# The Mamba layer's u times B on TensorE for three of sixteen states, with the h*C sum two slots behind the scan

## The reference

```python
def _selective_scan(x, dt, Bm, Cm, A, D):
    dA = jnp.exp(dt[..., None] * A)
    dBx = (dt * x)[..., None] * Bm[:, :, None, :]
    def step(h, inputs):
        dA_t, dBx_t, C_t = inputs
        h = dA_t * h + dBx_t
        y = jnp.einsum('bdn,bn->bd', h, C_t)
        return (h, y)
    ...
    return jnp.swapaxes(ys, 0, 1) + x * D[None, None, :]
```

## Time and profile before

| | before |
|---|---|
| time, median of 3 runs | 2807.88 us (2804.88 to 2809.41) |
| the profiled execution's own time | 2813.86 us |
| its span, first to last instruction | 2811.9 us |
| granted TensorE clock, mean of the span | 0.947 |
| the scans' stretch, about 334 to 1297 us of the span | some 963 us |

### The profile page before, as it was taken

How to read it: one execution, slowest core, us unless ns; L and a number is a source line. 1 busy time by engine, 2 the same in 40 slices (tenths; PEclk the granted TensorE clock), 3 DMA queues, 4 the chain that set the end, 5 groups by cost and what they waited for, 6 DMA issues and landing times. The chain is left out here.

```text
span 2811.9 us, 35676 instructions
## 1 busy us (share of the span) xinstructions
PE 2458.8 (87%) x10516; PEld 1557.5 (55%) x10516; DVE 2198.9 (78%) x4237; ACT 1732.2 (62%) x3055; POOL 1438.5 (51%) x1514
## 2 busy tenths in 40 slices
PE   7997587878888888877899599979999999997999
PEld 5876243333334334324677388855555555546887
DVE  7997589989999999997899555458877778755444
ACT  5876565557556666644777355536676767665555
POOL 2474698888888988885277450033232323310000
PEclk8999698999999999999999699989999999998999
DMA  2356222222222222222157310000000000001000
GB/s 83 79 158 122 69 76 70 72 69 74 68 73 76 75 74 74 75 76 66 35 149 137 95 34 1 1 15 1 1 1 1 1 1 1 1 1 42 8 8 15
DMA packets 99497, 146.06 MB, mean 52 GB/s; under 512 B 13036, under 2 KB 50540, under 8 KB 99124
## 3 DMA queue, kind: packets, MB, share of 16 engines
q1 hardware_dynamic: 82196, 98.60, 12.3%
q0 software_dynamic: 16608, 44.78, 7.5%
q10 hardware_dynamic: 512, 0.53, 0.1%
HBM read 124.98 MB, written 18.87 MB: 51 GB/s over the span
## 5 line engine op out<-in xcount | busy, mean ns | idle before, releaser
L1809 POOL TENSOR_TENSOR a_hc<-a_H,a_cb 128x512 f32<-128x512 f32 x512 | 619.6, 1231 | 136.6 <-DVE a_H L1672 129.2
L1464 PE MATMUL a_Y<-a_hc,ident 128*128 128x512 f32 x1024 | 541.7, 640 | 58.4 <-POOL a_hc L1809 49.8
L2165 ACT ACTIVATE a_pt<-a_W 128x512 f32<-128x512 f32 (+3 forms) x768 | 346.2, 496 | 202.8 <-PE a_W L2065 199.0
L1590 ACT ACTIVATE a_dA<-a_dt,a_aneg 128x512 f32<-128x512 f32 x512 | 342.8, 714 | 191.8 <-POOL a_dt L1828 100.6
L1464 PEld LDWEIGHTS a_Y<-a_hc,ident 128*128 128x128 f32 x1024 | 183.8, 197 | 313.2 <-POOL a_hc L1809 218.8
L1696 DVE TENSOR_TENSOR a_BX<-a_u,a_BX 128x1024 f32<-128x1024 f32 x256 | 308.2, 1209 | 38.3 <-PE a_BX L1398 27.3
L1672 DVE TENSOR_TENSOR_SCAN a_H<-a_dA,a_H,a_BX 128x512 f32<-128x512 f32 x256 | 312.1, 1261 | 2.5 <-ACT a_dA L1590 2.5
L2388 POOL TENSOR_SCALAR_AFFINE_SELECT a_pt<-a_pt 128x512 f32<-128x512 f32 x128 | 90.9, 710 | 423.1 <-ACT a_pt L2165 423.1
L1672 DVE TENSOR_TENSOR_SCAN a_H<-a_dA,a_BX 128x512 f32<-128x512 f32 x256 | 296.4, 1200 | 0.5 <-POOL a_hc L1809 0.5
L2251 DVE CUSTOM_DVE_ANT_0 a_masked<-a_W,a_mask 128x384 f32<-128x384 f32 (+3 forms) x512 | 231.7, 486 | 80.0 <-PE a_W L2052 77.8
L2065 PE MATMUL a_W<-a_Q,a_K 128*128 128x512 f32 (+3 forms) x768 | 283.6, 385 | 1.7 <-ACT a_pt L2165 1.6
(11 more groups left out here) (328 smaller groups left out, 5471.6 us busy)
## 6 DMA issues: line engine op xcount, KB each, us to landing
a_cb<-a_crow SPq DMA_DIRECT2D x256, 256.0 KB, 3.3
m_orows<-m_yt SPq DMA_DIRECT2D x46, 256.0 KB, 2.5
t_wst<-ternary_w SPq DMA_DIRECT2D x22, 256.0 KB, 2.9
m_xrows<-m_xn SPq DMA_DIRECT2D x16, 256.0 KB, 2.3
m_xg<-m_xrows,m_gidx POOLq DMA_INDIRECT x184, 3.3
out<-x SPq DMA_DIRECT2D x8, 256.0 KB, 2.3
m_wg<-moe_ws SPq DMA_DIRECT2D x2, 516.0 KB, 4.5
a_hc<-mamba_conv_rows SPq DMA_DIRECT2D x1, 1024.0 KB, 5.2
```

The source lines that it names most:

```text
L1464: pe.matmul(Y[:, h, :], ident[:], hc[:, g % HCRING, :], start=False, stop=v == NS - 1).then_inc(s_y, 1)
L1590: act.activation(dA[:, G % ARING, :], dt[:, b % 2, h, :], ACT.Exp, scale=aneg[:, d, h, v:v + 1]).then_inc(s_dA, 1)
L1809: pool.tensor_tensor(hc[:, G % HCRING, :], H[:, s, span], cb[:, v % RING, :], ALU.mult).then_inc(s_hc, 1)
L2165: act.activation(pt[:, u % PR, 0:BLK - r * P], W[:, 3 + u % 3, 0:BLK - r * P], ACT.Exp).then_inc(s_exp, 1)
```

## The change

1. In blocks 1 to 15 the states 7, 11 and 15 get their product from TensorE. `by_diagonal` multiplies u, transposed so that positions lie on the partitions (`uT`), by a diagonal matrix of B, 128 positions at a time: 8 float32 matmuls of 128 columns for a slot. No row is made for them, and VectorE has no product there. They stand on TensorE in slot v-1, behind the row and the use of `O`, ahead of the sums.
2. ScalarE makes the diagonals, 4 instructions of 128x128 in the place of `wi`, three slots ahead (`diagonal`). B on the positions' partitions (`bT`, in the place of `alog`) and `uT` come from three more uses of `O`: "bT" in slot 2 (t < 2) or 1, "uT" of half 1 in slot 4 or 3, and "uT" of half 0 of the next block in slot 14. ScalarE reads them.
3. `HCRING` goes from 8 to 6 halves.
4. `BEHIND = 2`: the sum of slot v-2 stands in TensorE's slot v, the last two in the next block's slots 0 and 1; `drain_y` and `gate` move from slot 1 to slot 2, and `open_y` with them.

```diff
-    HCRING = 8
+    HCRING = 6
...
+    BEHIND = 2
...
+    BY_PE = (7, 11, 15)
+
+    def on_pe(Q):
+
+        return Q >= NS and Q % NS in BY_PE
...
+        if has_scan(b):
+            uses.update({4 if t < 2 else 3: ("uT", 1, b), 2 if t < 2 else 1: ("bT", 0, b)})
+        if b + 1 < NB:
+            uses[14] = ("uT", 0, b + 1)
...
-                    if Q >= NB * NS:
+                    if Q >= NB * NS or on_pe(Q):
                         return
...
+                def by_diagonal(b, v):
+                    Q = b * NS + v
+                    if not on_pe(Q):
+                        return
+                    pe.wait_ge(s_dg, made_by(True, Q))
+                    pe.wait_ge(s_Oa, through("A", b, 4))
+                    for h in (1, 0):
+                        pe.wait_ge(s_scan, 2 * Q - 4 if h else 2 * Q - 3)
+                        out = BX[:, row_bank(Q) if h else half_bank(Q), :]
+                        for t in range(TPB):
+                            at = slice(t * P, (t + 1) * P)
+                            mm = pe.matmul(out[:, at], uT[:, h, at], wi[:, at], start=True, stop=True)
+                    mm.then_inc(s_tx, 1)
...
+                    elif kind == "uT":
+                        pe.wait_ge(s_u, 2 * tb + part + 1)
+                        for t in range(TPB):
+                            at = slice(t * P, (t + 1) * P)
+                            mm = pe.transpose(O[:, at], u[:, tb % 2, part, at], ident[:])
+                    elif kind == "bT":
+                        pe.wait_ge(s_dbl, tb + 1)
+                        for t in range(TPB):
+                            mm = pe.transpose(O[:, t * NS:(t + 1) * NS], dbl[0:NS, tb % 2, t * P:(t + 1) * P],
+                                              ident[0:NS, 0:NS])
...
-                        if has_scan(b) and v:
-                            add_y(b, v - 1)
-                    if has_scan(b):
-                        add_y(b, NS - 1)
+                        if has_scan(b) and v + 1 < NS:
+                            by_diagonal(b, v + 1)
+                        if has_scan(b) and v >= BEHIND:
+                            add_y(b, v - BEHIND)
+                        if has_scan(b - 1) and v < BEHIND:
+                            add_y(b - 1, NS - BEHIND + v)
...
+                def diagonal(b, v):
+                    Q = b * NS + v
+                    if not on_pe(Q):
+                        return
+                    act.wait_ge(s_Oa, through("A", b, 2))
+                    wait(act, s_tx, made_by(True, Q) - 1)
+                    for t in range(TPB):
+                        last = act.activation(wi[:, t * P:(t + 1) * P], ident[:], ACT.Copy,
+                                              scale=bT[:, t * NS + v:t * NS + v + 1])
+                    last.then_inc(s_dg, 1)
...
-                        if v == 1 and b > 0 and (b - 1) % 4 in (0, 1):
+                        if v == BEHIND and b > 0 and (b - 1) % 4 in (0, 1):
                             drain_y(b - 1)
...
                         if has_scan(b):
+                            if v + 3 < NS:
+                                diagonal(b, v + 3)
                             decay(b, v + LEAD)
...
-                            dve.wait_ge(s_B, Q + 1)
-                            wait(dve, s_scan, 2 * Q - 3)
-                            dve.tensor_tensor(both_banks(Q), u[:, b % 2, :, :],
-                                              BX[:, row_bank(Q), :].unsqueeze(1).broadcast_to([P, HALF, BLK]),
-                                              ALU.mult).then_inc(s_bx, 2)
+                            if not on_pe(Q):
+                                dve.wait_ge(s_B, made_by(False, Q))
+                                if Q and on_pe(Q - 1):
+                                    dve.wait_ge(s_tx, made_by(True, Q - 1))
+                                wait(dve, s_scan, 2 * Q - 3)
+                                dve.tensor_tensor(both_banks(Q), u[:, b % 2, :, :],
+                                                  BX[:, row_bank(Q), :].unsqueeze(1).broadcast_to([P, HALF, BLK]),
+                                                  ALU.mult).then_inc(s_bx, 2)
...
-                        if v == 1 and b > 0 and (b - 1) % 4 in (2, 3):
+                        if v == BEHIND and b > 0 and (b - 1) % 4 in (2, 3):
                             gate(b - 1)
```

More of the change, by code:

```diff
@@ L1219, in has_scan, with made_by @@
         return 0 <= b < NB
+    BY_PE = (7, 11, 15)
+    def on_pe(Q):
+        return Q >= NS and Q % NS in BY_PE
+    def made_by(pe, Q):
+        return sum(on_pe(q) == pe for q in range(Q + 1))
     def uses_of(b):
@@ L1228, in uses_of @@
                     10: ("z", 0, 0), 11: ("z", 1, 0),
-                    13: ("xp", 0, 2)}
+                    13: ("xp", 0, 2), 14: ("uT", 0, 1)}
         t = b % 4
@@ L1255, in silus_of @@
         return {9: (b + 2, None)} if b + 2 < NB else {}
-    COUNTED = {"O": ("T", "x", "z", "xp", "dt", "out"), "D": ("T", "out"), "A": ("x", "z", "xp", "dt")}
+    COUNTED = {"O": ("T", "x", "z", "xp", "dt", "out", "uT", "bT"), "D": ("T", "out"),
+               "A": ("x", "z", "xp", "dt", "uT", "bT")}
     ORDER = [(b, v, u[0]) for b in range(-1, NB + 1) for v, u in sorted(uses_of(b).items())]
@@ L1296, in mamba @@
         cb = sb("cb", [P, RING, BLK])
+        uT = sb("uT", [P, HALF, BLK])
         ab, ee, ln, uu = (sb(n, [P, BLK]) for n in ("ab", "ee", "ln", "uu"))
@@ L1323, in mamba @@
         s_B = sem("B")
+        s_dg, s_tx = sem("dg"), sem("tx")
         s_cb = [sem(f"cb{r}") for r in range(RING)]
@@ L1335, in mamba @@
                  (wo[:], w["out_proj"]))
+        bT = alog[:].rearrange("p e h n -> p (e h n)")
         sels = dA[0:DBC, 0:RING, :].rearrange("p a (n c) -> p (a n) c", c=P)
@@ L1396, in rows @@
                     if Q % NS == 2:
-                        pe.wait_ge(s_bx, 2 * Q - 2)
+                        pe.wait_ge(s_bx, 2 * made_by(False, Q - 2))
                     pe.matmul(BX[:, row_bank(Q), :], sel[:, Q % NS, :], bcs[:, Q // NS % 4, :], start=True, stop=True)\
                       .then_inc(s_B, 1)
+                def by_diagonal(b, v):
[11 more added lines that the diff above has]
+                    mm.then_inc(s_tx, 1)
                 def o_use(b, v, use):
@@ L1463, in add_y @@
                         pe.wait_ge(s_hc, b * UB + g + 1)
-                        pe.matmul(Y[:, h, :], ident[:], hc[:, g % HCRING, :],
+                        pe.matmul(Y[:, h, :], ident[:], hc[:, (b * UB + g) % HCRING, :],
                                   start=False, stop=v == NS - 1).then_inc(s_y, 1)
@@ L1535, in o_read @@
                         act.activation(zs[:, part, c, :], O[:], ACT.Copy).then_inc(s_Oa, 1)
+                    elif kind == "uT":
+                        wait(act, s_tx, made_by(True, tb * NS - 1))
+                        act.activation(uT[:, part, :], O[:], ACT.Copy).then_inc(s_Oa, 1)
+                    elif kind == "bT":
+                        act.activation(bT, O[:, 0:TPB * NS], ACT.Copy).then_inc(s_Oa, 1)
                     elif kind == "xp":
@@ L1660, in scan @@
                     dve.wait_ge(s_dA, G + 1)
-                    dve.wait_ge(s_bx, G + 1)
+                    if on_pe(G // 2):
+                        dve.wait_ge(s_tx, made_by(True, G // 2))
+                    else:
+                        dve.wait_ge(s_bx, 2 * made_by(False, G // 2))
                     wait(dve, s_hc, G - RING + 1)
```

## The result

The changed kernel takes 2819.55 us (median of 10 runs, 2813.61 to 2828.92); the kernel before, on the same chip, 2805.94 (10 runs, 2803.02 to 2809.41). The ratio is 1.0051, 95% interval 1.0043 to 1.0059: **slower by half a per cent**, some 14 us, where 6 us faster were forecast. The span of its profiled execution is 2821.4 us.

The account below looks back on a forecast made before the run. VectorE sets the pace in the scans, with TensorE locally full. Gains of 72.9 us (50.2 from products, 22.7 from waits) less losses of 67.2 leave 5.7 us faster: 2802 against 2807.9, range 2788 to 2819.

Parts of the forecast that it names:

- Slot 7 where t >= 2: Diagonal behind the convolution, about 4.6 us of waiting in five blocks, block 2 hidden: 23.0 us lost; where t < 2, 7.2.
- Slots 5 and 6 where t = 1: Rows come 0.75 and 1.35 us late in four blocks, as "bT" transposes wait for ScalarE: 8.4 us lost.
- The later sum: Waits for rows at slots 2 and 4 (9.8 and 8.5 us) and at the gate (4.4) go: 22.7 us gained.
- the gate: In blocks 4, 8 and 12 it waits for sums behind slot 1's convolution, 1.7 us each: 5.1 us lost.
- Slot by slot, at full clock: New waits for diagonals were priced at 1.95 us to their end; at half clock a diagonal would be near 3.6.
- the slack of a slot: VectorE's two scans, 2.24 or 2.36 us, less release, row, diagonal (1.95) and hand-over: about zero.
- slot 11: Where t < 2, xp before the diagonal, 8.4 us lost; where t >= 2 and in blocks 14 and 15, 0 to 0.1.
- slot 15: Four transposes before the diagonal, 0.5 us in eleven blocks, 5.5 lost; where t = 3, saved 1.1 lost three times, 3.3.
- u (10.5 before): GpSimd's u would not come sooner for the next block's first product: 6.3 us of the saved time lost.
- rival 2: TensorE's backlog carries on in slots 2 to 6 before a convolution, 16 us lost in eleven blocks: 2818; chance 0.28.
- Rival 1: TensorE has room, new matmuls overlap, only waits of fixed order stay (14.7 us): 2750; chance 0.05 with all between.
- Rival 3: GpSimd takes back 5 us more of the gain in blocks up to 5, where its fetches stand: 2807; chance 0.33.

Follow-up runs that it names:

- diag_first: The changed kernel with `by_diagonal` ahead of the row and the use of `O`, instead of behind both: 2777.02 us, ratio 0.9896 to the kernel before; repeated, 0.9907.
- sum_behind: The changed kernel with all products back on VectorE and the diagonals' transposes gone; later sum and ring of six kept: 2793.09 us, ratio 0.9955 to the kernel before.
- out_12: The changed kernel with the output projection of t = 3 in slot 12 instead of 13: 2820.09 us, ratio 1.0053 to the kernel before.
- sum_one: The changed kernel with the sum one slot behind instead of two, ring of six kept: 2837.92 us, ratio 1.0111 to the kernel before.
- Filler: The changed kernel with 8 extra, useless matmuls ahead of the row before slots 11 and 15, and 7 in the last two blocks: 2807.82 us, ratio 1.0008.
- row_diag_use: The changed kernel with the diagonal behind the row but ahead of the use of `O`: 2862.8 us against 2874.93 for the kernel before, ratio 0.9956.
- combined_four: combined with four states on TensorE, 8, 10, 12 and 15, instead of 9, 12 and 15: 2807.5 us, ratio 1.0006 to the kernel before.
- first_sums_ahead: diag_first with the last two sums of a block ahead of the use of `O` in slots 0 and 1: ratio 0.9899 to the kernel before.
- first_9_12_15: diag_first with states 9, 12 and 15 on TensorE instead of 7, 11 and 15: ratio 0.9913 to the kernel before.
- combined: diag_first with states 9, 12, 15, "out" in slot 12 and the last sums ahead where t = 0: 2780.17 us, ratio 0.9907 to the kernel before.

## Why the prediction was wrong

**What was right.** VectorE has 211 products and the diagonals 720 records; the 50.2 us are off VectorE (54 by busy time), and blocks 14 and 15 show it as soon as the diagonal is not in the way (4.1 and 3.4 us shorter in diag_first). Slot 7 where t >= 2: 5.0, 5.0, 5.65, 5.0 and 5.7 us in blocks 3, 6, 7, 10 and 11, 26.3 in all for 23.0; block 2, where all was to be hidden, waits 2.7; where t < 2 it is 7.4 for 7.2; the run without state 7 gives 15.4 back for 13.4. Slots 5 and 6 where t = 1: 7.4 for 8.4, each of the four pairs 0.69 and 1.16 us (1.0 more stands at slot 6 of blocks 7 and 11). That is in part luck: sum_behind has the 1.1 us of slot 6 without the "bT" transposes that the forecast put it down to. GpSimd and ScalarE hold up nothing new.

**The later sum was put too high.** 22.7 us of gain less 5.1 at the gate are 17.6; alone (sum_behind) it brought 12.9. The waits for rows fell by 15.3 us instead of 18.3. The larger error is the gate: 3.6 us on average in blocks 4, 8 and 12 instead of 1.7. The queue in front of it was counted rightly, each matmul at full clock; the rows of block 8 show the sum of slot 14 at 3.55 us instead of 1.88 and dt at 1.91 behind an idle stretch of 3.69, and that is more than the difference. So this error too is a price at full clock. In the changed kernel u is hardly waited for, and the gate costs 6.8 us.

**The step that failed** is the pricing "Slot by slot, at full clock". The prediction put the slack of a slot at "about zero" and then costed slot 11 where t >= 2 and blocks 14 and 15 at "0 to 0.1 us", and slot 15 at "0.5 in eleven blocks". A stretch with no slack at all was costed at the best price of the work in it, 1.95 us at full clock, though the other price, 3.6, stood beside it; 13 of the 45 diagonals took 2.35 to 3.58. The slack itself was right: where slot 11's diagonal kept the clock (blocks 2, 3, 7, 10 and 11), the product behind it waits 0.3 us or less. Measured against forecast, all from VectorE's waits of the changed kernel:

| place | forecast | measured | more |
|---|---|---|---|
| slot 7 (block 2 and blocks 14, 15: 4.8) | 23.0 + 7.2 | 38.5 | 8.3 |
| slot 11 | 8.4 | 21.7 | 13.3 |
| slot 15 | 5.5 + 3.3 | 26.2 | 17.4 |
| gate | 5.1 | 6.8 | 1.7 |
| u (10.5 before) | 10.5 + 6.3 | 4.7 | -12.1 |

The sum is 28.6 us. Waits for rows are 1.5 below the forecast (15.9 for 17.4: the 9.0 left from before and the 8.4 of t = 1), which leaves 27.1; the stage was forecast 5.7 shorter and came 17.8 longer, which is 23.5. Of the 3.6 us between, 2.4 are block 1's wait ahead of slot 15, which the kernel before has too; the rest stays unassigned. The last row is no gain of the change: VectorE is held up in slot 15 and so comes later to u (in out_12 the one wait goes and the other comes back).

**Why it was at 1.2 GHz.** Before, TensorE had a row to write in every slot and a sum whose h*C came late, which cut its idle time into pieces. The change takes a row out of the slot and makes the sum ready at once. What TensorE has left to wait for is then in one piece, 2.0 to 3.1 us, mostly ahead of the row of the next slot, and the diagonal comes right behind it.

Counted from the traces, from 735 us (in block 6) to the end of the stage: TensorE is idle for 70.6 us before and for 65.1 now, but before no piece is longer than 1.7 us, and now 16 are of 2 us or more. Neither part does it alone: sum_behind has 2 such pieces there and sum_one 7. The mean granted clock of 396 to 1308 us tells nothing of that: it was 0.96 in the kernel before and is 0.96 now. Over the stage TensorE is at its low level for 75.1 us before and 81.9 now. But before, the six low stretches from 735 us on all stand at the turn of a block (TensorE's slots 14 and 15), beside shorter idle pieces of up to 1.5 us, and VectorE waits for TensorE right behind two of them, 0.4 and 0.5 us. Now there are 13, 9 of them on a diagonal that VectorE waits for and 2 on the projection ahead of one.

Filler is the test: with the idle stretch filled, diagonals take 1.95 us, the clock of the stretch is 0.99, and 11.7 us come back, though TensorE does 41 us more work; the 15.1 us of excess length in the 13 slow diagonals and the 15.3 of the stage are of one size, though filler also gives the projection of slot 10 its clock back and lets other waits grow a little.

The Trainium skill (TensorE: Matmul & The Clock Gate, HAM oscillation — how this bites in real kernels) describes matmuls that come in bursts with idle gaps between them, each burst beginning at the low clock; there the gap is a transfer's. The rows of block 14 show the same with a gap of 2.23 us that a semaphore makes; those of block 10 show that a gap of that length does not always do it.

**What the clock does not explain, and one thing more that it does.** Filler still takes 2807.8 us and not diag_first's 2777.0. The rest is the queue: the uses of `O` ahead of the diagonal (27 us by row_diag_use, what it changes in the clock included; the forecast saw them in slots 7 and 11) and the late release of the row. In slot 11 where t < 2, 15.3 us were measured for 8.4. Block 1 did not hide its part, which is queue (1.9 us in filler too). The rest is the clock once more: in blocks 1, 8 and 12 xp itself runs at 1.2 GHz (3.3 to 3.6 us instead of 1.88), so that the product waits 3.6 or 3.7 us. In filler it waits 2.0 in blocks 8 and 12, as forecast. Block 12 of the changed kernel:

```profile
1117.06 0.79 PE L1417 MATMUL a_BX<-a_bcs,a_sel 128*128 128x512 f32 x1 [2.23 <-DVE a_H L1738]
1117.65 3.29 PE L1463 MATMUL a_O<-a_xs,a_xpw 128*72 128x512 f32 x4
1120.78 1.95 PE L1431 MATMUL a_BX<-a_wi,a_uT 128*128 128x128 f32 x16
```

**The rivals.** The time is nearest to rival 2's 2818, but its mechanism is not what happened: it wanted slots 2 to 6 of the blocks with convolutions to lose 16 us by hand-overs of `O`. Nothing is lost there beyond the 8.4 us at slots 5 and 6. It had the sign for another reason. Rival 1 (TensorE has room) falls with the waits of 5 us at slot 8's products, and with combined_four, where one more state makes products wait for TensorE's rows while the weight loads are busy 469 of 904 us. So the rule that the prediction weighed (the Trainium skill, Perfetto Trace Analysis, Identifying the Most-Contended Engine, where the weight loads' busy share, beside the share of peak flops, stands for headroom) would have misled by its weight loads for this kernel's float32 matmuls of 512 columns; the share of peak flops was not worked out. Rival 3, GpSimd, did not come about: u is waited for less, not more.

The prediction did say what would make it wrong, "a granted clock under 0.9 in the late blocks". It is 0.94 in blocks 14 and 15: even that mark was too coarse, since the mean over a block hides one diagonal.

**What stays open.** Filler shows that the clock goes up when the stretch is filled, and what it gives; how long TensorE may stand idle before the clock falls was not measured, nor why 2.23 us led to the low level in block 14 and not in block 10. In diag_first 27.6 us of waits for rows and 9.9 at the gate are left, and the orders tried around them (first_sums_ahead, first_9_12_15, combined) moved the waits without making the kernel faster; which of them would have to go together was not found. out_12 is at most 3 us shorter in the stage and no different in time. The ring of six was not run by itself.

## What to carry to other kernels

If an engine's new work is waited for in every slot, put it where its own inputs are ready, ahead of the instruction that waits for another engine, and not behind it: here that one move turned 0.5% slower into 1% faster. Here, taking a row out of TensorE's slot and making its sums ready sooner gathered its idle time in one piece. After such a change, look at what stands directly behind that piece, and price it at the low clock if somebody waits for it. A mean clock of a stage, or of a block, does not show this; the length of the same group of matmuls from block to block does.
